# Spectral mixing read in place: transformed images stored by frequency, GpSimd's column copies removed

## The reference

```python
# --- layer 1 ---
x = x + _L1_conv_ref(_gn(x), weight_real, weight_imag)     # weights: 32 x 32 x 128 x 65, real and imaginary
# in it:
x_ft   = symmetric_padding(rfftshift(rfft2(x, norm='forward')), ...)
out_ft = einsum('bixy,ioxy->boxy', x_ft, multiplier)       # a 32x32 complex matrix for every frequency
out    = irfft2(irfftshift(out_ft), norm='forward')
```

## Time and profile before

| | |
|---|---|
| median of 3 runs | 1137.1 us |
| profiled execution: its own time | 1137.38 us |
| its span | 1135.7 us |
| PE / PEld busy | 812.6 / 586.2 us |
| DVE busy | 734.2 us |
| ACT busy | 385.4 us |
| POOL busy | 331.6 us |
| granted TensorE clock, mean | 0.88 |

### The profile page before, as it was taken

The page is one execution under the profiler, slowest core; times in us unless marked ns, Lnnn a source line. Parts: engine busy times, 40 slices in busy tenths (PEclk is TensorE's granted clock), DMA queues, the critical chain, the costliest instruction groups (busy, mean ns, idle before and its releaser), DMA issues. The chain is left out here.

```text
span 1135.7 us, 36579 instructions
## 1 busy us (share of the span) xinstructions
PE 812.6 (72%) x16050; PEld 586.2 (52%) x16050; DVE 734.2 (65%) x1435; ACT 385.4 (34%) x850; POOL 331.6 (29%) x236
## 2 busy tenths in 40 slices
PE   0596057458999994699990599946777766776797
PEld 0464023212222221677770499836677666766686
DVE  5899869847888878555556799954544455553123
ACT  0253033202222225455553366622333333332121
POOL 0022010038999990011110000033443334442000
PEclk9998569859999997899995699968888888888899
DMA  9574160038455540333412376478999999999487
GB/s 359 119 188 97 38 162 1 0 108 327 161 192 171 176 130 0 92 91 95 152 20 81 89 193 180 137 158 193 267 270 272 265 263 264 264 265 222 140 246 218
DMA packets 270382, 189.36 MB, mean 167 GB/s; under 512 B 29060, under 2 KB 259173, under 8 KB 269221
## 3 DMA queue, kind: packets, MB, share of 16 engines
q1 hardware_dynamic: 189763, 131.47, 42.4%
q10 hardware_dynamic: 75426, 44.17, 16.1%
q0 software_dynamic: 5120, 12.75, 4.5%
HBM read 154.45 MB, written 33.07 MB: 165 GB/s over the span
## 5 line engine op out<-in xcount | busy, mean ns | idle before, releaser
L1929 PE MATMUL po<-pa,room 128*32 128x16 f32 x8320 | 146.7, 220 | 85.1 <-DMA room<-_L_conv_weight_imag_dram 58.2
L948 POOL TENSOR_TENSOR q<-wb,xb 128x1536 f32<-128x1536 f32 (+1 forms) x51 | 170.5, 3366 | 101.8 <-DMA wb<-wv 92.6
L1929 PEld LDWEIGHTS po<-pa,room 128*32 128x32 f32 x8320 | 144.2, 162 | 92.9 <-issue 81.6
L1018 DVE TENSOR_TENSOR q<-pw,xb 128x1536 f32<-128x1536 f32 (+1 forms) x85 | 140.7, 1703 | 26.0 <-PE acc L988 15.3
L988 PE MATMUL acc<-q,pt 128*32 128x384 f32 (+1 forms) x1088 | 105.0, 499 | 17.5 <-DVE q L1018 17.4
L2070 DVE TENSOR_TENSOR osl<-po,neg 128x128 f32<-128x128 f32 x64 | 18.4, 287 | 150.7 <-ACT neg L2003 150.7
L1882 POOL DMA_DIRECT2D os_<-osl x64 | 45.3, 713 | 183.8 <-DVE osl L2081 175.5
L1872 POOL COPY cols<-y 128x512 f32<-128x512 f32 x32 | 38.1, 1191 | 151.4 <-POOLq L1636 145.8
L1916 PE MATMUL px<-wbat,cols 128*32 128x130 f32 x2176 | 76.9, 295 | 4.1 <-DVE wbat L2041 3.0
L2003 ACT ACTIVATE neg<-po 128x272 f32<-128x272 f32 x32 | 12.7, 397 | 197.4 <-issue 182.3
L988 PEld LDWEIGHTS acc<-q,pt 128*32 128x32 f32 x1088 | 27.9, 110 | 93.1 <-issue 57.3
(11 more groups left out here) (326 smaller groups left out, 1528.5 us busy)
## 6 DMA issues: line engine op xcount, KB each, us to landing
room<-_L_conv_weight_real_dram ACTq DMA_DIRECT2D x32, 520.0 KB, 9.7
room<-_L_conv_weight_imag_dram ACTq DMA_DIRECT2D x32, 520.0 KB, 12.6
room<-_L_conv_weight_real_dram SPq DMA_DIRECT2D x32, 520.0 KB, 7.0
room<-_L_conv_weight_imag_dram SPq DMA_DIRECT2D x32, 520.0 KB, 10.4
xb<-xns SPq DMA_DIRECT2D x64, 192.0 KB, 3.1
wb<-wv SPq DMA_DIRECT2D x16, 576.0 KB, 5.9
yall<-in_x_dram SPq DMA_DIRECT2D x4, 2048.0 KB, 14.7
xd<-in_x_dram SPq DMA_DIRECT2D x16, 512.0 KB, 4.7
```

What stands on the lines that cost most here:

```text
L948: nc.gpsimd.tensor_tensor(q2[:, t % 2, :, :, 0:m], bc(weights(blk, n), 2, NB), spectra(blk), ALU.mult).then_inc(s_qp, 1)
L1018: V.tensor_tensor(q1[:, t % 2, :, :, 0:m], bc(pw[t % 4][:, 0:3 * m].rearrange("p (r m) -> p r m", r=3), 2, NB), spectra(blk), ALU.mult).th ...
L1929: e = nc.tensor.matmul(po[u][32 * g:32 * g + 32, 512 * q + 16 * m:512 * q + 16 * m + 16], wsl[u][:, :, q * KWF + KWF - 1 - kw], xsl[u][:, ...
```

## The change

`y1` is laid out by frequency, `[128, 65, 2, 128 images]`, so that the 128 images of one frequency and part lie side by side. ScalarE's copies and squares in stage 7 walk it with a step of 256 elements. `spectrum` reads `y1` itself; `cols`, `columns` and their semaphore are gone. In place of TensorE's loop the 32 chunks are written out, and the two spectra of chunks that don't exist are left out. The loop's counter appears in no address of the new `spectrum`: each chunk names its rows of `y1` directly.

```diff
-        y1 = fwd.enter_context(nc.sbuf_tensor("y1", [128, NI, 130], F32))
+        y1 = fwd.enter_context(nc.sbuf_tensor("y1", [128, KWF, 2, NI], F32))
...
-                    act.activation(y1[:, bass.ds(g * GI, GI), 0:65], v[:, :, 0:65], ACT.Copy)
-                    act.activation(y1[:, bass.ds(g * GI, GI), 66:129], v[:, :, 65:128], ACT.Copy).then_inc(s_e1, 1)
+                    even, odd = (y1[:, :, s, g * GI:g * GI + GI].rearrange("w k i -> w i k") for s in range(2))
+                    act.activation(even, v[:, :, 0:65], ACT.Copy)
+                    act.activation(odd[:, :, 1:64], v[:, :, 65:128], ACT.Copy).then_inc(s_e1, 1)
...
-                    act.activation(sq7[:, 0], y1[:, bass.ds(g * GI, GI), 0:64], ACT.Square, accum_out=en8[:, 0, bass.ds(g, 1)])
+                    act.activation(sq7[:, 0], even[:, :, 0:64], ACT.Square, accum_out=en8[:, 0, bass.ds(g, 1)])
...
-                V.memset(y1[:, :, 65:130:64], 0.0)
+                V.memset(y1[:, 0:65:64, 1, :], 0.0)
...
-                columns(0)
-                columns(1)
                 for v in range(2):
-                    pool.wait_ge(s_col, 2)
                     wait(pool, s_zero, v)
                     nc.gpsimd.memset(xsl[v], 0.0).then_inc(s_zero, 1)
                 pool.wait_ge(s_zero, 2)
                 for c_ in range(NCHK):
-                    columns(c_ + 2)
                     store(c_)
...
-                    pe.wait_ge(s_col, c_ + 1)
+                    if c_ == NCHK - 1:
+                        pe.wait_ge(s_b0, 1)
+                    wait(pe, s_xa, c_ - 1)
+                    wait(pe, s_xd, c_ - 1)
+                    upper = (SL * c_ + 1, SL * c_ + 2) if c_ < NCHK - 1 else (0, HH // 2 - 1)
+                    lower = (SL * c_ + 2, SL * c_ + 1)
...
-                                        m = nc.tensor.matmul(px[u][g:g + 32, o:o + 2 * KWF], cols[:, u, q if p == 0 else 3 - q, s, 32 * b:32 * b + 32],
+                                        m = nc.tensor.matmul(px[u][g:g + 32, o:o + 2 * KWF], y1[:, (upper, lower)[p][q], s, 32 * b:32 * b + 32],
...
-                with pe.Fori(0, NCHK // 2) as i:
-                    for u in range(2):
-                        mix(2 * i + u, u, i)
-                        spectrum(2 * i + u + 2, u)
+                for c_ in range(NCHK):
+                    mix(c_, c_ % 2, c_ // 2)
+                    if c_ + 2 < NCHK:
+                        spectrum(c_ + 2, c_ % 2)
```

More of the change, by code:

```diff
@@ L1714, in forward_copy @@
                     v = pf[:, :].rearrange("w (i k) -> w i k", i=GI)
-                    act.activation(y1[:, bass.ds(g * GI, GI), 0:65], v[:, :, 0:65], ACT.Copy)
-                    act.activation(y1[:, bass.ds(g * GI, GI), 66:129], v[:, :, 65:128], ACT.Copy).then_inc(s_e1, 1)
+                    even, odd = (y1[:, :, s, g * GI:g * GI + GI].rearrange("w k i -> w i k") for s in range(2))
+                    act.activation(even, v[:, :, 0:65], ACT.Copy)
+                    act.activation(odd[:, :, 1:64], v[:, :, 65:128], ACT.Copy).then_inc(s_e1, 1)
                     act.wait_ge(s_e1, g + 1)
                     wait(act, s_sq7, g)
-                    act.activation(sq7[:, 0], y1[:, bass.ds(g * GI, GI), 0:64], ACT.Square, accum_out=en8[:, 0, bass.ds(g, 1)])
-                    act.activation(sq7[:, 1, :, 0:63], y1[:, bass.ds(g * GI, GI), 66:129], ACT.Square, accum_out=en8[:, 1, bass.ds(g, 1)]).then_inc(s_sq7, 1)
+                    act.activation(sq7[:, 0], even[:, :, 0:64], ACT.Square, accum_out=en8[:, 0, bass.ds(g, 1)])
+                    act.activation(sq7[:, 1, :, 0:63], odd[:, :, 1:64], ACT.Square, accum_out=en8[:, 1, bass.ds(g, 1)]).then_inc(s_sq7, 1)
                 def body(b):
@@ L1775, in build @@
             xsl = [pflat[:, v * XS:(v + 1) * XS].rearrange("p (z b q c w) -> p z b q c w", z=2, b=NB, q=SL, c=2) for v in range(2)]
-            sq = sb("sq8", [128, NI, 2])
+            sq = sb("sq8", [128, 2, NI])
             en2 = sb("en8b", [128, NB, 2])
@@ L1784, in build @@
             eo, cf = sb("eo", [128, 128]), sb("cf", [128, 128])
-            cols = sb("cols", [128, 2, 4, 2, NI])
             osl = sb("osl", [128, 2, 2, SL, NB, 32])
@@ L1797, in build @@
             s_w = sems("weight_chunk_loaded", 2)
-            s_col, s_sp = sem("chunk_columns_copied"), sem("chunk_spectrum_done")
+            s_sp = sem("chunk_spectrum_done")
             s_xa, s_xd = sem("upper_rows_copied"), sem("lower_rows_copied")
@@ L1861, in _ @@
             def _(pool):
[L1862 to L1875, removed]
                 def store(c_):
@@ L2021, in _ @@
                 V = nc.vector
-                ch.link(V.reduce_sum(mo[:, 0, :], y1[:, :, 0].rearrange("w (b i) -> w b i", b=NB), axis=AX.X))
-                ch.link(V.tensor_tensor(sq[:, :, :], y1[:, :, 0:65:64], y1[:, :, 0:65:64], ALU.mult))
-                ch.link(V.reduce_sum(en2[:, :, :], sq[:, :, :].rearrange("w (b i) k -> w b k i", b=NB), axis=AX.X))
+                ch.link(V.reduce_sum(mo[:, 0, :], y1[:, 0, 0, :].rearrange("w (b i) -> w b i", b=NB), axis=AX.X))
+                ch.link(V.tensor_tensor(sq[:, :, :], y1[:, 0:65:64, 0, :], y1[:, 0:65:64, 0, :], ALU.mult))
+                ch.link(V.reduce_sum(en2[:, :, :], sq[:, :, :].rearrange("w k (b i) -> w b k i", b=NB), axis=AX.X))
                 ch.link(V.reduce_sum(mo[:, 1, :], en8[:, 0, :].rearrange("w (b q) -> w b q", b=NB), axis=AX.X))
@@ L2041, in _ @@
                 V.tensor_tensor(wbat[:, :, :], bc(wide[:, :], 1, NB), bc(gs[:, 2, :], 2, 4 * KWF), ALU.mult).then_inc(s_wb, 1)
-                y0 = y1[:, :, 0].rearrange("w (b i) -> w b i", b=NB)
+                y0 = y1[:, 0, 0, :].rearrange("w (b i) -> w b i", b=NB)
                 V.tensor_tensor(y0, y0, bc(gs[:, 0, :], 2, NT), ALU.subtract).then_inc(s_b0, 1)
```

## The result

The changed kernel takes 1248.16 us (median of 4 runs, 1245.72 to 1251.41) against 1136.82 before: 1.098 times as long, 95% interval 1.0955 to 1.101. The profiled execution took 1247.78 us, its span is 1246.1 (1135.7 before), so 110.4 us are to be found in the trace. They are nearly all in the mixing stage.

What follows compares the result with a forecast made beforehand. The prediction took the weights' transfers as the bound before and code fetching after the change: 126.6 - 1 - 2 = +123.6 us on 1137.38 gives 1261 us, range 1205 to 1306.

Steps and rivals of the forecast that it cites:

- The bound before: Mixing stage: the weights' transfers set its rate, 8.98 us a chunk; GpSimd's copies hide behind them, worth 1 us at most.
- The code as the pace: Mixing loop written out: every chunk fetches 2.53 blocks of instructions, 13.5 us a chunk instead of 8.98, +126.6 us; 84%.
- in those 9.0 us 1.34 blocks arrive: Step for one mixing chunk: blocks take 6.7 us during 9.0 us of weight transfer, the other 1.19 take 3.6 each.
- The idle price of 3.6: Mixing stage: time for one block of TensorE's code with DMA engines nearly idle, mean of 3.45 and 3.73 us.
- The lean towards the one chunk seen: Mixing chunk: 13.5 us taken, near the worked-out 13.3 and a little towards the 14.2 seen in the loop's first turn.
- The last two chunks: End of the mixing stage, no spectrum behind them: 18.8 us against 20.0 before, -1 us.
- The head: Start of the mixing stage: GpSimd clears sooner without its copies, TensorE's spectra start some 2 us sooner; -2 us, bounds 0 and -4.
- ScalarE's steps: Stage 7, copies and squares with steps of 256 elements: no price, 0 us, judged by VectorE's clearing.
- The sum for the doubling: Stage 7: four ScalarE operations at double time end 1.7 us later, costing nothing but 1 to 2 us behind the last group.
- the rival of three times the time: Stage 7: ScalarE's operations at three times the time become the bound, +31 us over 16 groups, 1292 us; 4%.
- Code in time: Mixing stage: code is fetched early enough, chunks stay at 8.98 us, only the start's gain remains, 1134 us; 7%.
- Blocks at the idle rate: Mixing stage: blocks come in 3.6 to 4 us even under load, 9.1 to 10 us a chunk, 1138 to 1163 us; 5%.

## Why the prediction was right

**The bound before.** Weights set the pace; shown by the loop with few weights, whose chunk falls from 8.92 to 6.63 us, and by the loop with two spectra, whose chunk stays (8.94).

**The code as the pace.** Foretold +126.6 us for 28 chunks at 13.5 us, measured +108.3 at 12.84. The cause is shown by doing it alone, and by undoing it together with GpSimd's copies. The size was off by 0.66 us a chunk. The count of 2.53 blocks and both prices hold nearly: idle 3.73 us (802.31 to 806.04) and loaded 6.7 us (the block of 816.87, counted from where the one before it was entered, 128 multiplications after 806.04; 52 of the 179 from 809.24, so at about 810.2). What failed is the step "in those 9.0 us 1.34 blocks arrive". One block in a chunk comes at the loaded price, 6.95 us between packets, and the other 1.53 at 3.84, which makes 12.83. In the stretch shown, the time of one block, 810.2 to 816.87, falls wholly into the transfers (808.2 to 817.4); the block entered at 810.2, 4.1 us after the one before it, was there in time. A second step failed that made no difference to the sum: "a block is used up in 2.4 us, so TensorE would stand at every block's end". A block with a spectrum in it at the lower clock takes 4.1 us (806.04 to 810.2) and is left without a stop, which helps to explain the 50 stops for 71 blocks. The idle price of 3.6 came from two values; a third in the same rows, 766.55 to 770.53, is 3.98, and the measured mean is 3.84. The lean towards the one chunk seen, 14.2 us, made the size worse: 13.3 was worked out.

**The last two chunks.** -1 foretold, +1.2 measured: the mix at 1156.74 waited 2.3 us for its weights, which the sum had ready. It gave them 1.6 + 9.0 us; those of the last chunk were issued at 1142.20 and ended the wait 14.5 us later. The kernel before had the same (issued at 1033.31, mix at 1048.65), so a row of before could have told it.

**The head.** -2 foretold; the stage's head is 2.3 us shorter, for the reason given. The first mix starts only 0.2 us earlier (760.99 for 761.22) and not at 759, since the stage starts 1.9 us later. So the -2 of the sum was not there: mix(1) ends 0.7 us later than before.

**ScalarE's steps.** Taken at 0 by the nearest row, VectorE's clearing, which was the wrong row to go by: the operations take 1.8 times as long. The sign that L1715 and L1720 stay near 600 ns failed with it. The price lay between the bounds, near the doubling: hidden, but for "1 to 2 us behind the last group". There the copies and squares take 4.08 us for 2.46, 1.6 more, and with a start 0.3 us later the stage ends 1.9 later. The sum for the doubling has a slip: four operations of 600 ns, doubled, are 2.4 us more and not 1.7 (and the rival of three times the time would have cost 53 us and not 31); the measured 1.8 times gives 1.9 in a group in mid-stage (672.62 to 676.95). The group still takes 5.67 us, now with ScalarE at work for 5.51 of them (674.34 to 680.01); by that it had 0.16 us left before it would have been the bound.

**The total.** It was foretold 13 us too high. The chunks were 18.3 us too high; the start of the stage (2.7 us), the last two chunks (2.2) and the rest (0.2) were too low and made good 5 of them, which is luck and not part of the reasoning.

**The rivals.** Code in time is refuted by 141.7 us of "issue". That the stops belong to the loop's entry is refuted by the straight code. Blocks at the idle rate would have given 9.1 to 10 us a chunk; that is what the run with few weights shows, and only that one. A packet of code moves at 803.5, within the block entered at 802.31, so code comes while TensorE multiplies; that hides little of its time where a block is used up in 2.4 us and the packets follow one another after 3.8 to 7 us. Written out, the same work takes 1252.45 us against 1140.84.

## What to carry to other kernels

Count the instructions that an engine issues per microsecond before writing a loop out: here the matmuls of a mix, four instructions each, used up a block of 256 in 2.4 us (128 multiplications in 2.36 us from 802.31), and a new block took 3.7 us with the DMA engines nearly idle and about 6.9 us beside the weights' transfers. The loop before, whose body of 5.1 blocks was kept, had no stop on "issue" from 786 to 1053 us, after its first turn, where the changed kernel has 54 between 780 and 1170; look at the instruction queue's packets and at stops in mid-run with no semaphore, and at the first turn of a loop, which here showed nearly what all turns became without it (14.2 us for its one chunk, 12.84 measured). And take away only what is late: GpSimd's copies were hidden but for 2 us at the head, and the price paid here for removing them was the loop.

## What the runs showed of the hardware

- Each matmul of mix and spectrum is two weight loads and two multiplications in the trace: 8320 of each for 4160 matmuls, 2176 of each for 1088.
- Of TensorE's loops, bodies of 5.1 and 6.1 blocks (44 and 46 packets in all) are kept from turn to turn; one of 10.1 blocks is fetched again in each turn, 12 blocks a turn, and was slower (1288.89 us) than straight code (1252.45).
- In straight code one block a chunk comes 6.8 to 7.1 us after the one before it, while the weights are in transfer, and the others after 3.8 to 4.0; with an eighth of the weights they come after 3.8 in the mean, none later than 5.
- ScalarE with steps of 1024 bytes: 1084 ns for 520 columns where it was 608, whether the steps are in what it writes or in what it reads (1132 for 602).
- GpSimd's copy of 512 columns: 1.14 us with steps of 520 bytes in its source, 0.61 without.
- VectorE's TENSOR_SCALAR on 4 columns takes up to 1.87 us beside GpSimd's clearing, and its TENSOR_TENSOR and TENSOR_SCALAR on 4 to 8 columns 1.02 to 1.05 us beside GpSimd's copies, for 0.16 to 0.17 us alone; TENSOR_TENSOR beside the clearing takes 0.16.
